# Routed expert tiles: the down products moved directly behind the up products, the six turns put in a row, waits spread over the products

## What is computed

```python
def _L0_ffn_ref(x, gate_w, w1, b1, w2, b2, shared_w1, shared_b1, shared_w2, shared_b2):
    logits = xf @ gate_w
    top_logits, top_idx = jax.lax.top_k(logits, K)          # K = 2 of E = 8
    top_gates = jax.nn.softmax(top_logits, axis=-1)
    ...
    h = gelu(jnp.einsum('nd,edh->neh', xf, w1) + b1)        # D 512 -> H 256
    out_e = jnp.einsum('neh,ehd->ned', h, w2) + b2          # H 256 -> D 512
    routed = jnp.einsum('ne,ned->nd', gates, out_e)
    shared = gelu(xf @ shared_w1 + shared_b1) @ shared_w2 + shared_b2
    return (routed + shared).reshape(B, S, D)
```

## Time and profile before

| | |
|---|---|
| median of 3 runs | 2452.65 us (2449.98 to 2454.01) |
| the profiled execution, its own time | 2464.65 us |
| its span, first to last instruction | 2462.8 us |
| PE busy | 2333.6 us (95%) |
| DVE busy | 1660.4 us (67%) |
| ACT busy | 1137.2 us (46%) |
| POOL busy | 657.8 us (27%) |
| mean granted TensorE clock | 0.977 of 2.4 GHz |

### The profile page before, as it was taken

The page is one execution under the profiler, slowest core; times in us unless marked ns, Lnnn a source line. Parts: engine busy times, 40 slices in busy tenths (PEclk is TensorE's granted clock), DMA queues, the critical chain, the costliest instruction groups (busy, mean ns, idle before and its releaser), DMA issues. The chain is left out here.

```text
span 2462.8 us, 41627 instructions
## 1 busy us (share of the span) xinstructions
PE 2333.6 (95%) x13062; PEld 1992.7 (81%) x13062; DVE 1660.4 (67%) x3852; ACT 1137.2 (46%) x2697; POOL 657.8 (27%) x545
## 2 busy tenths in 40 slices
PE   6999999999999999978999789999999999888997
PEld 6888898989898988866887568888888888756885
DVE  7555555555546555675665748888988898874666
ACT  4444434443434344442332436666666666542334
POOL 1111111110101011125221324444444443343223
PEclk9999999999999999988999889999999999998999
DMA  4524333233342524215884100000000000127865
GB/s 166 179 92 161 109 127 141 104 139 130 106 163 91 178 91 164 88 67 214 299 276 175 48 10 10 18 9 18 9 18 9 9 18 9 35 75 248 276 235 229
DMA packets 103300, 279.70 MB, mean 114 GB/s; under 512 B 9096, under 2 KB 11528, under 8 KB 97568
## 3 DMA queue, kind: packets, MB, share of 16 engines
q1 hardware_dynamic: 82336, 222.81, 25.9%
q0 software_dynamic: 11360, 37.76, 4.0%
q10 hardware_dynamic: 9504, 17.85, 2.2%
HBM read 133.40 MB, written 144.98 MB: 113 GB/s over the span
## 5 line engine op out<-in xcount | busy, mean ns | idle before, releaser
L609 DVE SCALAR_TENSOR_TENSOR x<-bank,inv,x 128x512 f32<-128x512 f32 x512 | 361.7, 744 | 173.3 <-PE bank L76 171.1
L619 DVE TENSOR_TENSOR hq_lo<-bank,hq_hi 128x512 fp32r<-128x512 f32 (+1 forms) x320 | 201.2, 637 | 267.3 <-ACT hq_hi L555 102.4
L74 PE MATMUL bank<-xT_hi,w_hi 128*128 128x512 f32 x864 | 350.7, 406 | 18.1 <-POOL w_lo L700 6.3
L497 ACT ACTIVATE s<-s,top 128x128 f32<-128x128 f32 (+3 forms) x512 | 282.1, 552 | 156.0 <-DVE top L601 156.0
L76 PE MATMUL bank<-xT_hi,w_lo 128*128 128x512 f32 x864 | 344.2, 398 | 0.0
L75 PE MATMUL bank<-xT_lo,w_hi 128*128 128x512 f32 x864 | 344.0, 398 | 0.0
L563 ACT ACTIVATE hq_hi<-bank 128x512 fp32r<-128x512 f32 x128 | 76.5, 597 | 388.1 <-PE bank L76 388.1
L74 PE MATMUL bank<-wo_hi,hq_hi 128*128 128x512 f32 (+1 forms) x576 | 234.1, 406 | 0.7 <-DVE xT_lo L178 0.7
L75 PE MATMUL bank<-wo_lo,hq_hi 128*128 128x512 f32 (+1 forms) x576 | 228.6, 397 | 0.0
L76 PE MATMUL bank<-wo_hi,hq_lo 128*128 128x512 f32 (+1 forms) x576 | 228.1, 396 | 0.0
L601 DVE CUSTOM_DVE_ANT_0 s<-bank,mask 128x128 f32<-128x128 f32 (+3 forms) x512 | 216.7, 479 | 4.3 <-PE bank L76 4.3
(11 more groups left out here) (282 smaller groups left out, 5851.3 us busy)
## 6 DMA issues: line engine op xcount, KB each, us to landing
sorted_x<-blank SPq DMA_DIRECT2D x48, 1584.0 KB, 11.4
arena<-split_w SPq DMA_DIRECT2D x32, 1024.0 KB
split_w<-arena SPq DMA_DIRECT2D x48, 512.0 KB, 3.0
raw<-dram_wr SPq DMA_DIRECT2D x24, 512.0 KB, 5.8
w_raw<-dram_wa SPq DMA_DIRECT2D x16, 512.0 KB, 3.7
arrived<-routed_y SPq DMA_DIRECT2D x8, 1024.0 KB, 9.2
row_pt_hi<-sorted_x ACTq DMA_DIRECT2D x22, 264.0 KB
row_pt_lo<-sorted_x ACTq DMA_DIRECT2D x20, 264.0 KB
```

Of the source, the lines that this page charges most:

```text
L74: nc.tensor.matmul(out, hi, mov_hi, start=first, stop=False)
L497: nc.scalar.activation(at, at, ACT.Exp, bias=m.top[:, b, t:t + 1], scale=-1.0, accum_out=m.rowsum[:, b, t:t + 1]).then_inc(a.probs_ready, 1)
L609: nc.vector.scalar_tensor_tensor(out=xt, in0=m.bank[6 + t % 2][:, :], scalar=m.inv[:, b, t:t + 1], in1=xt, op0=ALU.mult, op1=ALU.add).then ...
L619: return nc.vector.tensor_tensor(out, bank, hi.bitcast(F32), ALU.subtract).then_inc(done, 1)
```

## The change

`expert_of` keeps only the register load; its waits go to a new `input_for`. `route_down` issues its products one by one: the register load for the next tile now stands before the third of the six products, and the waits for the next tile's input stand on the sixth. In the loop, `route_down(i - 1)` stands directly behind `route_up(i)`, and `turn(i + 2)` after it, directly ahead of `turn_hidden(i)`. Behind the loop, the last `route_down` moves between the two halves of up(5). The lists of ACT, DVE, POOL and SP are unchanged.

```diff
--- before.py
+++ after.py
@@ -1229,12 +1229,14 @@
 
     def expert_of(i):
 
-        expert = pe.value_load(m.tab[0:1, E_AT + i:E_AT + i + 1], min_val=0, max_val=E - 1)
+        return pe.value_load(m.tab[0:1, E_AT + i:E_AT + i + 1], min_val=0, max_val=E - 1)
+
+    def input_for(i):
+
         pe.wait_ge(rt.xs_lo, i0 + i + 1)
         ge(pe, rt.biased, i0 + i - 1)
         if i < 2:
             pe.wait_ge(f.gelu_done, KH * (s0 + B + 1))
-        return expert
 
     def slot_for(expert):
 
@@ -1262,7 +1264,7 @@
                                        m.ident[:, :])
         last.then_inc(rt.h_turned, 1)
 
-    def route_down(i, slot, within=nothing):
+    def route_down(i, slot, more=False):
         expert = None
         pe.wait_ge(rt.h_lo, i0 + i + 1)
         ge(pe, rt.y_out, i0 + i - 1)
@@ -1272,10 +1274,14 @@
             at = slice(k * P, k * P + P)
             w = slot[:, 2048 + k * D:2048 + k * D + D]
             wl = slot[:, 3072 + k * D:3072 + k * D + D]
-            last = product(nc, m.bank[OUT_BANK[i % 2]][:, :], m.hT[HI][:, i % 2, at], m.hT[LO][:, i % 2, at],
-                           w, wl, k == 0, k == KH - 1)
-            if k == 0:
-                expert = within(i + 2)
+            out, h_hi, h_lo = m.bank[OUT_BANK[i % 2]][:, :], m.hT[HI][:, i % 2, at], m.hT[LO][:, i % 2, at]
+            nc.tensor.matmul(out, h_hi, w, start=k == 0, stop=False)
+            nc.tensor.matmul(out, h_hi, wl, start=False, stop=False)
+            if more and k == 0:
+                expert = expert_of(i + 2)
+            if more and k == KH - 1:
+                input_for(i + 2)
+            last = nc.tensor.matmul(out, h_lo, w, start=False, stop=k == KH - 1)
         last.then_inc(rt.y_done, 1)
         return expert
 
@@ -1329,23 +1335,25 @@
     down(B, (0, 1))
 
     pe.wait_ge(rt.tables_out, TABLES_OUT * (L + 1))
+    input_for(0)
     before, slot, coming = None, slot_for(expert_of(0)), None
     for i in range(TILES):
         route_up(i, slot)
+        if i:
+            expert = route_down(i - 1, before, i + 1 < TILES)
         if i + 2 < TILES:
             turn(i + 2)
-        if i:
-            expert = route_down(i - 1, before, expert_of if i + 1 < TILES else nothing)
-        else:
+        if not i:
             down(B, (2, 3))
             expert = expert_of(1)
+            input_for(1)
         if i + 1 < TILES:
             coming = slot_for(expert)
         turn_hidden(i)
         before, slot = slot, coming
     up(B + 1, 1, 0)
+    route_down(TILES - 1, before)
     up(B + 1, 1, 1)
-    route_down(TILES - 1, before)
 
     up(B + 2, 2, 0)
     up(B + 2, 2, 1)
```

## The result

| | before | after |
|---|---|---|
| median | 2453.0 us (4 runs) | 2564.12 us (2561.04 to 2565.03, 4 runs) |
| ratio to before | 1 | 1.0453, 95% interval 1.044 to 1.0466 |
| span of the profiled execution | 2462.8 us | 2562.3 us |
| turn_hidden(1) to turn_hidden(37), both layers | 272.35 us | 193.38 + 194.68 = 388.06 us |

The change costs 111.1 us. Forecast were 2565 us. The two loops alone are 115.7 us longer (forecast 114.2). The spans differ by only 99.5 us, mostly because the profiled execution of before was slow elsewhere. From its last turn_hidden of the first layer to the first of the second it took 950.5 us, where three other kernels with the same code there (`e3_turn_only`, `e4_load_only`, `e10_before_lo_first`) took 940.2 to 941.2, and its turn_hidden(1) lies 3.7 us later than that of the change.

A forecast was written before the change was run, and what follows sets the result against it. A chain of waits over two tiles, not PE's own work, was taken to set the pace. 36 x 5.35 + 1.0 - 0.35 a layer, 386.5 against 272.35, gave +114.2; less 2.3, +111.9: median 2565 us, range 2530 to 2605.

The forecast's parts named there:

- The chain of two tiles: Routed loop before: down waits through the input of the tile two ahead; 7.53 us for two tiles, 3.77 each.
- the ring of one tile: Changed loop: down(i-1), turn(i+2), input_hi, input_lo, mark, output, hidden_lo, down(i) close a chain every tile; 5.35 us.
- The terms: Changed loop: down 1.85, turn to input_hi 0.67, to input_lo 0.61, to hidden_lo's end 2.07, to down 0.15 us.
- The hole that I kept at 0.37: Register load within down: PE hole in every tile, taken as 0.37 us; bounds nothing and 0.37 + 0.25.
- Tile 3: Routed loop, tile 3: the exponential of the gates lengthens the wait of down(3); 1.0 us added.
- The last down product: Behind each loop: results come earlier, saving DVE's 1.72 us and ACT's 0.55 us of waits; -2.3 us, no more.
- rival 1: Routed loops: PE's idle stretches lower the clock; 2670 us if it stays down, 2617 if half the time; chance 12%.
- The pulled weight loads: Down in the loop: weight loads pulled ahead would remove the register load's hole; 4.98 us a tile, about 2538 us.
- Rival 2: Routed loops: down never waits and tiles run at PE's own pace, 3.48 us; 2429 us; chance 4%.
- Rival 3: Whole kernel: the slower tile is absorbed, no change beyond 0.2%; chance 2%.

The follow-up runs named there:

- e3_turn_only: Kernel before, with only turn(i+2) moved behind down(i-1); 2564.22 us, ratio 1.0455.
- e4_load_only: Changed kernel with turn and the last down product put back, leaving the earlier register load and the waits on the sixth product; 2452.66 us, ratio 0.9997.
- e10_before_lo_first: Kernel before, with DVE's hidden_lo(i) ahead of output(i-1) and PE's list untouched; 2447.92 us, ratio 0.9976.
- e12_lo_first_dve_load: e11_lo_first_last_down with DVE's register load for the next tile directly behind bias(i); 2433.94 us, ratio 0.9926.
- e5_last_down_only: Kernel before, with only the last routed down product moved ahead of the second half of up(5); 2449.82 us, ratio 0.9986.
- e6_load_ahead: Changed kernel, with PE's register load for the next tile ahead of the down product and its wait for hidden_lo; 2539.4 us, ratio 1.0349.
- e9_hidden_dve_load: e1_hidden_first with DVE's register load for the next tile moved directly behind bias(i); 2442.97 us, ratio 0.9955.
- e1_hidden_first: Changed kernel with ACT and DVE doing the hidden values ahead of the input, PE's list kept; 2481.17 us, ratio 1.0121.
- e11_lo_first_last_down: e10_before_lo_first with the last routed down product moved as in the change; 2442.49 us, ratio 0.9959.

## Why the prediction was right

- **The chain of two tiles as what bound the kernel before.** Shown in direction, and not as the only thing in the way. `e10_before_lo_first` left PE's list untouched and took output out of the chain: that gave 4.0 us in the loops, where the chain alone would have given up to 21.8 (272.35 - 250.6). `e12_lo_first_dve_load` moved DVE's register load as well and came to 257.39 us, 15.0 less. So a second round, on DVE and ACT, lay close behind the chain, and the prediction had not seen it. It does not enter the sum for the change, where the ring of one tile is longer.
- **Turn behind down closes the ring in every tile.** `e3_turn_only` gives the loss, `e4_load_only` none of it. Two links were taken out one by one, and each moved the loops by what the ring says: 42.4 us for output (forecast 41), 24.2 us for the register load (forecast 24.5).
- **The terms.** 5.35 us a tile forecast, 5.30 measured: down 1.82 for 1.85, turn to input_hi 0.63 for 0.67. The hole that I kept at 0.37 against an upper bound of 0.62 is 0.34.
- **Tile 3 was mis-sized, and for more than one reason.** I added 1.0 us to it. It took 7.70 and 7.71 us instead of 5.30, so 2.4 more in each layer. The rows of the first layer, then of the second, and ACT's own register load (line 1416) in each:

```profile
1187.80 1.28 ACT L1472 ACT_TABLE_LOAD   x1 [1.21 <-DVE ids L1517]
...
1190.68 0.49 PE L1278 MATMUL bank<-arena,hq_hi 128*128 x1 [3.09 <-DVE hq_lo L1523]
...
1192.66 1.03 PE L1226 MATMUL bank<-ident,row_vw_hi 128*128 128x128 f32 x4
...
2326.04 1.28 ACT L1472 ACT_TABLE_LOAD   x1 [0.50 <-issue]
...
2326.18 0.20 DVE L1514 TENSOR_SCALAR first<-row_pt_lo,esc 128x1 f32<-128x1 f32 x1
...
2328.95 0.50 PE L1278 MATMUL bank<-arena,hq_hi 128*128 x1 [2.40 <-DVE hq_lo L1523]
...
2331.61 1.05 PE L1226 MATMUL bank<-ident,row_vw_hi 128*128 128x128 f32 x4
```
```profile
L1416 ACTq TENSOR_LOAD <-tab x1: 982/982/982, 1186.1 to 1186.1; - x1
L1416 ACTq TENSOR_LOAD <-tab x1: 273/273/273, 2325.0 to 2325.0; - x1
```

In the second layer PE waits 2.40 us instead of 1.24. These 1.16 us are the exponential, near the 1.0 that I took. The step that failed is that I let nothing else happen there. The other 1.25 us are the clock, which had fallen: down to turn takes 2.66 us instead of 1.82, and turn to turn_hidden 0.84 instead of 0.43. In the first layer PE waits 3.09 us, 1.85 more, and the clock takes the other 0.56. Of the 1.85, 0.7 come from ACT's register load ahead of the exponential, which took 0.98 us there and 0.27 in the second layer; why is open. (The profile puts ACT's wait there down to DVE's mark, but in the second layer the table load begins before mark does.)

In the sum of the loops, against the forecast, the ring gave 3.6 us less, tile 3 gave 2.8 more, the tile of 6.90 us gave 1.6 more, and small things 0.8 more. The result is 1.6 us from the forecast, closer than the terms themselves, and that is luck.
- **The last down product.** Forecast -2.3 with nothing more to be had; `e5_last_down_only` gives about -3.4, with an interval that holds both. The second wait of ACT, 0.97 us, was the row that I missed. A slip that enters nothing: 12 products by 1.48 us for six are 2.96, not 2.8.
- **The clock (rival 1)** fell, but only in places. PE stands 1.24 us in each regular tile and the clock reads 1.00 there; the mean over the loops is 0.99 and 0.98. It fell three times, each time behind a longer wait and for some 3 us, to 0.50 (1.2 GHz): in tile 3 of both layers (waits of 3.09 and 2.40 us), and in one regular tile of the second layer, where output on DVE began 0.33 us late and PE waited 1.58 us. The rows are the windows of the second layer in tile 3 and in that tile, and its wait:

```profile
2330.00:2332.00 2.00, 2.00 (x6) 1.51 (x7) 0.00 (x0) 0.17 (x1) 0.00 (x0) 0.50 0.75 264
2412.00:2414.00 2.00, 2.00 (x9) 1.68 (x8) 0.00 (x0) 0.04 (x1) 0.00 (x0) 0.50 0.78 259
```
```profile
2410.22 0.49 PE L1278 MATMUL bank<-arena,hq_hi 128*128 x1 [1.58 <-DVE hq_lo L1523]
```

That tile took 6.90 us, 1.6 more than its neighbours. `e3_turn_only` falls in the same three places, there behind a wait of 1.59 us in the regular tile. In `e6_load_ahead` PE waited 1.59 us in that tile too (it took 5.33 us), and the clock stayed up, so the length of the wait alone does not decide it, and what does is open. The ring ran close to rival 1 all the same. In the kernel before, and in every kernel whose loops take under 275 us, the clock stays up in both loops. The swinging clock that TensorE: Matmul & The Clock Gate of the Trainium skill describes for short idle stretches between groups of products (A second HAM failure mode: psum-queue depth-cycling) does not show in the regular tiles, whose hole is 1.24 us each; the trace shows three single falls.
- **The pulled weight loads.** The prediction gave the time (2538 us) for the case that the rule of TensorE: Matmul & The Clock Gate in the Trainium skill (Part 2, step 1), weight loads pulled ahead of products, also covers a weight load with a register load in front of it. In this trace it does not: the hole of 0.34 us is there, and `e6_load_ahead` gets 0.33 us a tile back when the register load is put ahead of the wait.
- **Rival 2, the faster side,** asked for a tile at PE's own pace with the changed list of PE. With the lists of DVE and ACT as they were, which the prediction named against it, it did not come about. With other lists it nearly did (3.66 us in `e9_hidden_dve_load`); 3.46 to 3.48 us a tile came only with the old list of PE, in `e12_lo_first_dve_load`. Rival 3, no change, is out by the ratio.

## What to carry to other kernels

Before moving work on one engine, write down the lists of the others and follow the wait around: if an in-order engine does A, then B, and the move makes A need what B feeds, the two engines lock into a ring of one tile, however idle they both are. Busy shares say nothing of it (DVE was at 64% before and 45% after in this loop); the period of one tile does, and its terms could be read from the trace of before. The cheap repair is in the order of the engine that looks idle: here one line and one register load moved on DVE, without any change to PE's loop, take 15.0 us out of the loops of the kernel before. With the last down product moved too, that is the fastest kernel.

When engines wait in every round, look at the granted clock in each odd tile and not only at its mean over the loop: means of 0.99 and 0.98 over the two loops hid three falls.

## What the hardware showed that I had not expected

A register load queued behind an instruction that waits costs its engine a hole, on DVE as on PE: 0.67 us ahead of bias in `e1_hidden_first`, 0.20 to 0.37 in `e10_before_lo_first`, 0.34 on PE with the change. Three pairs of kernels show it, each with one load moved: 24.2 us in the loops on PE, 35.6 and 11.8 on DVE. In `e6_load_ahead` the loads themselves took longer, and it did not matter (source views of the load over a whole launch, with the change and in `e6_load_ahead`; ns as least, median, most):

```profile
L1232 PEldq TENSOR_LOAD <-tab x78: 295/301/495, 1163.4 to 2507.3; - x78
L1232 PEldq TENSOR_LOAD <-tab x78: 297/494/1132, 1163.7 to 2482.6; - x78
```

Why the median is 494 ns there and 301 with the change stays open. So do the long tiles of up to 4.4 us in `e10_before_lo_first` beyond the hole; the register load accounts for most of them, since the loops went from 269.19 us (`e11_lo_first_last_down`) to 257.39 with it moved, but not for the last 7 us over PE's own 250.6, of which the extra of tile 3 is a part.
